# A graph convolution and soft mixture of experts on one core: the combining weights turned by the DMA engines instead of TensorE

## The reference

```
x = x + gcn(relu(gcn(layernorm(x), W1)), W2)
xn = l2norm(layernorm(x)); logits = xn @ (scale * l2norm(phi))   # 6250 x 1024
d_w = softmax over the 32 slots of an expert; c_w = softmax over all 1024
slots = d_w.T @ xn                                               # 1024 x 768
h  = gelu(slots @ w1 + b1); eo = h @ w2 + b2                     # per expert, 1024 x 768
x = x + c_w @ eo                                                 # 6250 x 768
```

## Time and profile before

| | |
|---|---|
| Median of three runs | 3811.48 us (3809.83 to 3813.83) |
| The profiled execution | 3808.86 us, span 3807.1 us |
| TensorE products busy | 3299.6 us, 87% of the span |
| TensorE weight loads busy | 2087.9 us, 55% |
| VectorE busy | 1811.5 us, 48% |
| ScalarE busy | 1093.5 us, 29% |
| GpSimd busy | 1727.0 us, 45% |
| Mean granted clock of TensorE | 0.966 of full |

### The profile page before, as it was taken

The page is one execution under the profiler, slowest core; times in us unless marked ns, Lnnn a source line. Parts: engine busy times, 40 slices in busy tenths (PEclk is TensorE's granted clock), DMA queues, the critical chain, the costliest instruction groups (busy, mean ns, idle before and its releaser), DMA issues. The chain is left out here.

```text
span 3807.1 us, 63490 instructions
## 1 busy us (share of the span) xinstructions
PE 3299.6 (87%) x20875; PEld 2087.9 (55%) x20875; DVE 1811.5 (48%) x2830; ACT 1093.5 (29%) x1313; POOL 1727.0 (45%) x1692
## 2 busy tenths in 40 slices
PE   7204999999999999969999999999999954479998
PEld 6102666666666666645556556556556521146665
DVE  8685233333333333227777777777777740021111
ACT  3652222222222222214344344344344310011110
POOL 0103766666666666547666656666666400000000
PEclk9997999999999999989999999999999987789999
DMA  8264988888888888759888888888888649934443
GB/s 341 95 264 148 319 287 288 287 284 291 288 282 291 289 280 292 256 186 349 293 302 298 298 294 299 296 295 298 307 288 300 233 149 351 321 130 151 151 152 126
DMA packets 265456, 994.14 MB, mean 261 GB/s; under 512 B 38306, under 2 KB 67260, under 8 KB 265200
## 3 DMA queue, kind: packets, MB, share of 16 engines
q0 software_dynamic: 133728, 656.12, 50.1%
q1 hardware_dynamic: 131472, 334.56, 24.7%
HBM read 867.64 MB, written 122.89 MB: 260 GB/s over the span
## 5 line engine op out<-in xcount | busy, mean ns | idle before, releaser
L1139 POOL DMA_INDIRECT m_ring<-table,idx x833 | 877.8, 1054 | 539.8 <-PE m_part L1300 308.6
L872 POOL DMA_INDIRECT a_ring<-table,idx x833 | 833.7, 1001 | 480.7 <-PE a_part L976 300.5
L1300 PE MATMUL m_part<-m_ring,m_pick 128*128 128x512 f16 (+1 forms) x3332 | 598.3, 329 | 11.4 <-DMA m_ring<-table,idx 10.2
L976 PE MATMUL a_part<-a_ring,a_pick 128*128 128x512 f16 (+1 forms) x3332 | 580.4, 327 | 10.2 <-DMA a_ring<-table,idx 9.3
L1300 PEld LDWEIGHTS m_part<-m_ring,m_pick 128*128 128x128 f16 x3332 | 418.9, 142 | 155.2 <-issue 23.3
L976 PEld LDWEIGHTS a_part<-a_ring,a_pick 128*128 128x128 f16 x3332 | 413.6, 142 | 137.8 <-issue 18.9
L1315 PE MATMUL m_ps_s<-m_dw,m_xn 128*128 128x512 f16 x1764 | 428.8, 380 | 12.1 <-DVE slots L1198 12.1
L1626 PE MATMUL c_po<-c_eh,c_cT 128*128 128x512 f16 (+1 forms) x1568 | 328.8, 327 | 12.3 <-DVE c_cT L1595 12.3
L1328 PE MATMUL m_ps_l<-phi_h,m_xT 128*128 128x512 f16 x1176 | 309.8, 379 | 0.3 <-issue 0.2
L1315 PEld LDWEIGHTS m_ps_s<-m_dw,m_xn 128*128 128x128 f16 x1764 | 171.5, 98 | 183.7 <-issue 19.4
L1198 DVE TENSOR_TENSOR slots<-slots,m_ps_s 128x512 f32<-128x512 f32 x288 | 196.5, 683 | 150.5 <-PE m_ps_s L1315 150.5
(11 more groups left out here) (354 smaller groups left out, 4204.4 us busy)
## 6 DMA issues: line engine op xcount, KB each, us to landing
e_w1s<-in_L_ffn_w_dram SPq DMA_DIRECT2D x32, 1152.0 KB, 14.8
e_w2s<-in_L_ffn_w_dram SPq DMA_DIRECT2D x32, 1152.0 KB, 13.6
cw_dram<-m_cst SPq DMA_DIRECT2D x49, 512.0 KB
c_cw<-cw_dram SPq DMA_DIRECT2D x49, 512.0 KB, 4.7
x_pad<-xs SPq DMA_DIRECT2D x7, 2688.0 KB, 24.0
table<-stage SPq DMA_DIRECT2D x49, 384.0 KB, 2.3
a_own<-table SPq DMA_DIRECT2D x49, 384.0 KB, 4.3
table<-a_stage SPq DMA_DIRECT2D x49, 384.0 KB, 2.8
```

Of the source, the lines that this page charges most:

```text
L872: pool.indirect_dma_start(out=ring[:, t, :], out_offset=None, in_=table, in_offset=bass.IndirectOffsetOnAxis(ap=idx[:, k:k + 1], axis=0)). ...
L976: mm = nc.tensor.matmul(part[:, bass.ds(to + a, z - a)], pick[:, i % 2, :, t], ring[:, t, half * D + a:half * D + z], start=False, stop=(t ...
L1139: pool.indirect_dma_start(out=ring[:, t, :], out_offset=None, in_=table, in_offset=bass.IndirectOffsetOnAxis(ap=idx[:, n:n + 1], axis=0)). ...
L1300: mm = nc.tensor.matmul(part[:, bass.ds(off + at, e - f)], pick[:, i % 2, :, t], ring[:, n % RING, half * D + f:half * D + e], start=False ...
```

## The change

The weights come from DRAM already turned. SP's load becomes a transposing transfer from `cw_dram` straight into `cT`, which now has 16 squares of 128 by 128 in each of two buffers (the high part's 8, then the low part's 8). The buffer `cw`, the PSUM tile `ps_t`, TensorE's turns, ScalarE's and VectorE's copies and their three semaphores go. The transfer of block i waits until the products of block i - 2 have ended, for it writes the buffer that they read. TensorE waits once for `el`, then for each block for its transfer and for the addition of block i - 2. VectorE only adds.

```diff
-            combine(nc, eo, cw_dram, x2_dram, ident16, out)
+            combine(nc, eo, cw_dram, x2_dram, out)
...
-        cw = sb("cw", [P, 2, 2 * K], F16)
-        cT = sb("cT", [P, 2, 2, K], F16)
+        cT = sb("cT", [P, 2, 2 * KC, P], F16)
...
-        ps_t = ctx.enter_context(nc.psum_tensor("c_pt", [P, 2, 2, 1024], F16))
...
                         if exists(i, NBR):
-                            wait(sp, turned, i - 1)
-                            sp.dma_start(cw[:, s, :], cw_dram[bass.ds(i * P, P), :]).then_inc(cw_in[s], 16)
+                            wait(sp, prod, i - 1)
+                            sp.dma_start(cT[:, s], cw_dram[bass.ds(i * P, P), :], transpose=True).then_inc(turned_in[s], 16)
                             wait(sp, summed, i - 1)
...
-                            act.wait_ge(turned, i + 1)
-                            wait(act, prod, i - 1)
-                            nc.scalar.activation(cT[:, s, 0, :], ps_t[:, s, 0, :], ACT.Copy).then_inc(hi_back, 1)
...
-                            v.wait_ge(turned, i + 1)
-                            wait(v, prod, i - 1)
-                            v.tensor_copy(cT[:, s, 1, :], ps_t[:, s, 1, :]).then_inc(lo_back, 1)
-                        b = i - 1
-                        if exists(b, NBR):
-                            v.wait_ge(prod, b + 1)
-                            v.wait_ge(x_in[1 - s], 16 * (j + s))
-                            wait(v, stored[1 - s], 16 * (j + s - 1))
-                            v.scalar_tensor_tensor(ob[:, 1 - s, :], ps_o[:, 1 - s, 0:D], inv[:, 0:1], xb[:, 1 - s, :], ALU.mult, ALU.add).then_inc(summed, 1)
+                            v.wait_ge(prod, i + 1)
+                            v.wait_ge(x_in[s], 16 * (j + 1))
+                            wait(v, stored[s], 16 * j)
+                            v.scalar_tensor_tensor(ob[:, s, :], ps_o[:, s, 0:D], inv[:, 0:1], xb[:, s, :], ALU.mult, ALU.add).then_inc(summed, 1)
...
             def _(pe):
+                pe.wait_ge(e_lo, 1)
+
...
-                            pe.wait_ge(cw_in[s], 16 * (j + 1))
-                            wait(pe, hi_back, i - 1)
-                            wait(pe, lo_back, i - 1)
-                            for half in range(2):
-                                for c in range(KC):
-                                    mm = nc.tensor.transpose(ps_t[:, s, half, c * P:(c + 1) * P], cw[:, s, half * K + c * P:half * K + (c + 1) * P], ident16[:, :])
-                            mm.then_inc(turned, 1)
-                        b = i - 1
-                        if exists(b, NBR):
-                            pe.wait_ge(hi_back, b + 1)
-                            pe.wait_ge(lo_back, b + 1)
-                            pe.wait_ge(e_lo, 1)
-                            wait(pe, summed, b - 1)
+                            pe.wait_ge(turned_in[s], 16 * (j + 1))
+                            wait(pe, summed, i - 1)
                             for c in range(KC):
                                 for half, ee in ((0, eh), (0, el), (1, eh)):
                                     for a, e in ((0, 512), (512, D)):
-                                        mm = nc.tensor.matmul(ps_o[:, 1 - s, a:e], cT[:, 1 - s, half, c * P:(c + 1) * P], ee[:, c, a:e],
+                                        mm = nc.tensor.matmul(ps_o[:, s, a:e], cT[:, s, half * KC + c, :], ee[:, c, a:e],
                                                               start=(c == 0 and half == 0 and ee is eh), stop=(c == KC - 1 and half == 1))
```

More of the change, by code:

```diff
@@ L1503, in _, with combine @@
                 rounds(pe, n, body, head=2)
-def combine(nc, eo, cw_dram, x2_dram, ident16, out):
+def combine(nc, eo, cw_dram, x2_dram, out):
     with ExitStack() as ctx:
@@ L1524, in combine @@
         sc = sb("sc", [P, 1], F32)
-        cw = sb("cw", [P, 2, 2 * K], F16)
-        cT = sb("cT", [P, 2, 2, K], F16)
+        cT = sb("cT", [P, 2, 2 * KC, P], F16)
         xb = sb("xb", [P, 2, D], F32)
         ob = sb("ob", [P, 2, D], F32)
-        ps_t = ctx.enter_context(nc.psum_tensor("c_pt", [P, 2, 2, 1024], F16))
         ps_o = ctx.enter_context(nc.psum_tensor("c_po", [P, 2, 1024], F32))
-        maxed, allmax, scaled, e_hi, e_lo, dve, turned, hi_back, lo_back, prod, summed = (sem("c_" + n) for n in (
-            "maxed", "allmax", "scaled", "e_hi", "e_lo", "dve", "turned", "hi_back", "lo_back", "prod", "summed"))
-        cw_in = [sem("c_cw0"), sem("c_cw1")]
+        maxed, allmax, scaled, e_hi, e_lo, dve, prod, summed = (sem("c_" + n) for n in (
+            "maxed", "allmax", "scaled", "e_hi", "e_lo", "dve", "prod", "summed"))
+        turned_in = [sem("c_cw0"), sem("c_cw1")]
         x_in = [sem("c_x0"), sem("c_x1")]
@@ L1566, in _ @@
                 nc.scalar.activation(eh[:, :, :], eo[:, :, :], ACT.Copy, scale=sc[:, 0:1]).then_inc(e_hi, 1)
[L1568 to L1571, removed]
-                            act.wait_ge(turned, i + 1)
-                            wait(act, prod, i - 1)
-                            nc.scalar.activation(cT[:, s, 0, :], ps_t[:, s, 0, :], ACT.Copy).then_inc(hi_back, 1)
-                rounds(act, n, body, head=2)
             @block.vector
```

## The result

The changed kernel takes 3766.96 us (median of 4 runs, 3764.16 to 3767.86) against 3810.65 us before (median of 4): a ratio of 0.9883, 95% interval 0.9866 to 0.9900, 43.7 us less. Forecast were 3769.1 us and 42.4 us less.

A forecast was written before the change was run, and what follows sets the result against it. TensorE was taken to bound the combine stage, at 8.69 us a block. Turns (41.8 us) and the first copy (0.6 us) gave 42.4 us, the transfer being hidden: 3811.48 - 42.4 = 3769.1 us, range 3763 to 3995.

The forecast's parts named there:

- its turns are worth their time in the chain: Combine stage: 16 transposes a block cost TensorE 0.89 us; 47 of 49 groups lie on the path, 41.8 us gained.
- The first copy: Stage start: VectorE's copy of block 0's weights, ahead of TensorE's first product, goes; 0.6 us gained.
- The ramp of the clock: Stage start: TensorE's clock rises from half to full; TensorE idles before its first product either way, so no change.
- The copies in the loop: ScalarE's 1022 ns and VectorE's 680 ns copies per block: both engines idle over 7 us a block, so worth nothing.
- Engine time of the transposing transfer: Combine stage, per block: 128 pieces of 256 B on each DMA engine at 17.7 ns, 2.3 us, hidden.
- a line between two rows: Price of 256 B pieces, 17.7 ns, between profile rows of 512 B (28.5 ns) and 16 B (7.5 ns).
- Landing: Weights' transfer in the combine stage: lands 4.2 us after issue, at most 6.7, against 7.6 us available; hidden.
- SP's issue: One transposing issue per block on SP; even at 5.3 us, sixteen plain ones, SP would be in time.
- Late by a little: Rival: weights land over 7.6 us after issue, so each product waits; 3769 to 3811 us, middle 3785; chance 0.09.
- Small strips: Rival: the transposing transfer writes 32 B strips, 7.7 us of every engine a block; 3877 us, up to 3995; chance 0.18.
- Squares one after another: Rival: a block's 16 squares follow each other, each with part of its latency, 20 us; 4455 us total; chance 0.11.

The follow-up runs named there:

- the late issue: The changed kernel with each transposing transfer issued only after the product of the block before has ended, so that nothing hides it: 1.0669 of the kernel before.

## Why the prediction was right

- **TensorE bounds the stage, so its turns are worth their time in the chain.** Right. 47 x 0.89 = 41.8 us was the main term; putting the turns back alone restored the time before.
- **The first copy, forecast at 0.6 us.** Right: 0.65 us.
- **The ramp of the clock at no change.** Missed by about 1.2 us, the main part of what the main stretch gained beyond the forecast (43.4 measured, 41.8 forecast; 0.3 to 0.4 us are left over). The first block's products took 10.81 us before and take 9.6 now (3371.44 to about 3381.0): the clock came back 3.2 us after they began, at 3374.6, where before it took over 5 us. The shorter time repeats: in seven other traces whose block 0 is the changed kernel's it is 9.5 to 9.8 us. Of the kernel before there is one trace. There TensorE had turned 32 squares first and then stood idle for 12.3 us, now it idles 22.2 us; the kernel with one transfer per square took 10.5 us. Why it is shorter stays open.
- **The copies in the loop at nothing.** Right: put back, without TensorE waiting for them, they cost nothing.
- **Engine time of the transposing transfer: 2.3 us from a line between two rows.** Measured 62.6% of 7.80 us = 4.9 us for the three transfers, less the 2.4 us that the prediction puts down to the other two by their bytes: 2.5 us, or 19.5 ns per 256 B packet for the 17.7 taken. Three per block gave 10.0 us a block, which agrees. That a straight line between a load of 512 B rows and a store of 16 B rows came so near is partly luck, and the forecast did not need it: with two transfers a block the time was still almost the same.
- **Landing 4.2 us, at most 6.7, of 7.6 available.** Right to 0.3 us: measured 4.5 (4.4 to 4.7).
- **SP's issue.** It was bounded at 5.3 us and not priced; it is 2.0 to 2.7 us, six to eight plain issues. It did not matter, since it lies inside the landing time and SP has 7.80 us.
- **Rivals.** Late by a little: 3.1 us were to spare. Small strips: the queue shows pieces of 256 B, 80941 small packets for 38 blocks, 2048 a block and some of the other transfers' own, where 32 B strips would have made 16384 a block; and the engine time is 2.5 us, not 7.7. The warning given with this rival, that idle time lowers the clock, held for the late issue, 1.9 us a block. Squares one after another: not so in one instruction; as sixteen instructions the price of 20 us a block came true, by SP's issue and not by the latency that the rival named.

## What to carry to other kernels

Where TensorE bounds a stage and the operands come from DRAM anyway, let the transfer turn them: price the turn by its piece of the chain, not by its own busy time, and check that landing and engine time fit into one period of the cover. Make one transposing transfer of many squares, for the issue of a single square cost 1.15 us and that of sixteen 2.35. And keep it a whole product ahead, since bare it cost 4.4 us a block and 1.9 us of clock on top.

## What the runs showed of the hardware

- A transposing issue holds SP for 1.15 us for one 128x128 f16 square and 2.0 to 2.7 us for sixteen; a plain issue of the same 512 KB holds it 0.33 us.
- 512 KB turned on the way hold the 16 engines for 2.5 us, plain for 1.8 (62.6 and 54.2% of 7.80 us, each less 2.4). With nothing to hide them TensorE waited 4.5 us a block for the turned and 4.2 us for the plain.
- An idle TensorE of 4.4 us per 9.7 us of products brought the granted clock to 0.88, and the lower pace began only about 1 us after the products had started again.
- Chips differ: the same kernel took 3810, 3970 and 4005 us, while the products of the last stage took the same time on each (383.5 to 384.0 us). The difference lies ahead of that stage: it began at 3351 us in the changed kernel's profile, and at 3511 us in that of the version with the copies put back, whose program is the same up to there. Why is open.
